# Gate products of a mixture-of-experts layer with the gate's weights standing, a bridge of unit-matrix products, and one more shared unit ahead of the routed ones

## The reference, cut to what matters

```python
t = layernorm(h).reshape(-1, d)                      # 3136 x 128
hs = gelu(einsum('td,nfd->ntf', t, sw1) + sb1)       # 2 shared experts, F = 512
shared = einsum('ntf,ndf->td', hs, sw2) + sb2.sum(0)
logits = t @ gate_w.T + gate_b                       # 3136 x 8
probs = softmax(logits)
top_v, top_i = top_k(probs, 2)
hr = gelu(einsum('td,efd->etf', t, rw1) + rb1)
oe = einsum('etf,edf->etd', hr, rw2) + rb2
routed = sum over the 2 chosen experts of top_v * oe
out = h + shared + routed
```

## Time and profile before

| | |
|---|---|
| median of 3 runs | 440.13 us (439.99 to 445.27) |
| profiled execution | 444.05 us, its span 442.1 us |
| PE busy | 364.2 us, 82% of the span |
| PEld, DVE, ACT, POOL busy | 299.8, 183.0, 205.5 and 174.1 us |
| granted clock, mean of the span | 0.883 |

### The profile page before, as it was taken

One profiled execution on the slowest core, in us unless ns is written; L12 is line 12 of the kernel. 1 busy time (PEld: TensorE's weight loads), 2 busy tenths in 40 slices (PEclk: granted clock), 3 DMA queues, 4 the chain that ended last, 5 costly groups with the idle time before them and its releaser, 6 DMA issues.

```text
span 442.1 us, 7120 instructions
## 1 busy us (share of the span) xinstructions
PE 364.2 (82%) x2490; PEld 299.8 (68%) x2490; DVE 183.0 (41%) x579; ACT 205.5 (46%) x424; POOL 174.1 (39%) x226
## 2 busy tenths in 40 slices
PE   0596998998967895839899999999999999989400
PEld 0465856666655784739777878988988988988300
DVE  0473485737769202392787221121121121121166
ACT  2660647837351631445563244554454445455153
POOL 7015134255221230062000357767767767654100
PEclk9995799998995697955798899999999999999855
DMA  8962046930010341022003015425435444455185
GB/s 209 265 191 74 16 131 165 312 128 0 1 71 40 122 150 60 1 74 73 0 33 130 19 42 210 159 101 212 156 128 183 161 146 166 172 173 187 29 278 149
DMA packets 22168, 54.38 MB, mean 123 GB/s; under 512 B 4551, under 2 KB 10109, under 8 KB 22137
## 3 DMA queue, kind: packets, MB, share of 16 engines
q1 hardware_dynamic: 17625, 46.25, 31.8%
q0 software_dynamic: 3968, 7.41, 6.0%
q10 hardware_dynamic: 544, 0.33, 0.4%
HBM read 28.10 MB, written 6.93 MB: 79 GB/s over the span
## 4 chain that ended last, share of the span: by engine, by line
PE 52%; issue 15%; DVE 12%; DMA 8%; POOL 4%; POOLq 3%; DVEq 3%; ACT 3%; SPq 1%; ACTq 0%
PE bank L1528 11%; PE bank L1505 11%; PE bank L1515 8%; DMA Xc<-in_x 3%; PE bank L1267 3%; PE bank L1300 3%; DVE dT L848 2%; PE bank L1480 2%; PE bank L1485 2%; PE bank L1486 2%; PE bank L1487 2%; DMA out<-osb 2%; DMA Tt<-kpad 1%; PE bank L1355 1%; PE bank L1563 1%
## 5 line engine op out<-in xcount | busy, mean ns | idle before, releaser
L633 POOL DMA_INDIRECT xg<-yd,take x56 | 54.5, 974 | 64.1 <-DVE give L1186 47.3
L784 ACT ACTIVATE gf<-bank,wb 128x256 f32<-128x256 f32 (+1 forms) x128 | 51.3, 447 | 52.6 <-PE bank L1505 52.6
L640 POOL DMA_INDIRECT rd<-og,give x56 | 55.2, 986 | 41.4 <-DVE og L1200 28.9
L1528 PE MATMUL bank<-wb,gf 128*128 128x128 f32 x448 | 55.4, 275 | 1.0 <-DVE og L1200 1.0
L1505 PE MATMUL bank<-x,wb 128*128 128x256 f32 (+1 forms) x256 | 54.0, 354 | 2.1 <-issue 1.2
L1528 PEld LDWEIGHTS bank<-wb,gf 128*128 128x128 f32 x448 | 53.2, 192 | 1.5 <-DVE og L1200 1.5
L784 ACT ACTIVATE gf<-bank,vcol 128x392 f32<-128x392 f32 x64 | 35.2, 588 | 36.5 <-PE bank L1487 36.5
L1505 PEld LDWEIGHTS bank<-x,wb 128*128 128x128 f32 x256 | 43.3, 191 | 9.3 <-issue 1.4
L1515 PE MATMUL bank<-gf,ws 128*128 128x392 f32 x128 | 44.8, 492 | 0.0
L1193 DVE COPY x<-bank 128x256 f32<-128x256 f32 (+1 forms) x32 | 12.5, 391 | 65.4 <-PE bank L1563 65.3
L1300 PE MATMUL bank<-patchT,Wp 128*128 128x392 f32 x96 | 38.4, 527 | 0.0
(11 more groups left out here) (266 smaller groups left out, 627.7 us busy)
## 6 DMA issues: line engine op xcount, KB each, us to landing
wb<-tab SPq DMA_DIRECT2D x32, 578.0 KB, 3.3
Xc<-in_x SPq DMA_DIRECT2D x12, 784.0 KB, 6.8
rk<-rd SPq DMA_DIRECT2D x8, 392.0 KB
Tt<-kpad SPq DMA_DIRECT2D x8, 300.1 KB
raw<-in_L_ffn_rw SPq DMA_DIRECT2D x1, 2048.0 KB, 10.2
out<-osb SPq DMA_DIRECT2D x8, 196.0 KB
Tt<-kpad SPq DMA_DIRECT2D x2, 600.2 KB
Tt<-kpad SPq DMA_DIRECT2D x1, 1200.5 KB
```

Of the source, the lines that this page charges most:

```text
L633: G.indirect_dma_start(out=xg[i % AHEAD][:, t, :], out_offset=None, in_=yd[:, :], in_offset=bass.IndirectOffsetOnAxis(ap=take[:, at:at + 1 ...
L640: G.indirect_dma_start(out=rd[:, :], out_offset=bass.IndirectOffsetOnAxis(ap=give[:, at:at + 1], axis=0), in_=og[i % 2][:, t, :], in_offse ...
L784: nc.scalar.activation(gf[q % 2][:, o, 0:width(q)], bank[o][:, 0:width(q)], ACT.Gelu, bias=bias1(n, o)).then_inc(act_done, 1)
L1528: last = MM(bank[7][:, D * t:D * (t + 1)], gf[q % 2][:, o, 128 * t:128 * (t + 1)], wb[i % WB][:, FO + F + o * D:FO + F + (o + 1) * D], sta ...
```

## The change

The gate's weights (`gwT`, 128 by 8) stand, and a chunk's 392 tokens move: one product a chunk instead of four. Its output is 8 rows, in one of four groups of 32 rows of a bank; four chunks share a bank. DVE copies each of the two banks to SBUF (`lgt`), TensorE transposes them, four transposes a bank, and DVE adds the bias in two instructions. Both copies stand in `choose()`, behind `low_y(0)`; the transposes stand between the last gate product and `up(0)`. 28 products of the unit matrix, whose result nobody reads, stand ahead of the first transpose of y. The wait for the expert weights moves ahead of the first gate product. `LEAD` is 7 and `S_TURN` is 4; `count_places()` stands behind `up(2)` instead of `up(1)`. With these constants, the last shared unit stands after block 26, and five routed blocks end the list.

```diff
+IDLE_Y = 28
-LEAD = 6
+LEAD = 7
-S_TURN = 3
+S_TURN = 4
+        lgt = [place(f"lgt{i}", [128, GT], "y") for i in range(2)]
             def choose():
-                dve.wait_ge(gate_done, NG)
-                V.tensor_tensor(lg[:, :, :], bank[7][0:PAIR, 0:NPAIR * E].rearrange("p (g e) -> p g e", e=E),
-                                gbb[:, :].unsqueeze(1).broadcast_to([PAIR, NPAIR, E]), ALU.add)
+                for b in range(2):
+                    dve.wait_ge(gate_done, 4 * (b + 1))
+                    V.tensor_copy(lgt[b][:, :], bank[b][:, 0:GT]).then_inc(lgt_ready, 1)
+                dve.wait_ge(logits_T, 2)
+                for b in range(2):
+                    V.tensor_tensor(lg[:, NPAIR // 2 * b:NPAIR // 2 * (b + 1), :].rearrange("t (c g) e -> t c g e", g=GP),
+                                    bank[4 + 3 * b][0:PAIR, :].rearrange("t (g c e) -> t c g e", g=GP, c=4)[:, :, :, 0:E],
+                                    gbb[:, :].unsqueeze(1).unsqueeze(1).broadcast_to([PAIR, 4, GP, E]), ALU.add).then_inc(logits_read, 1)
             def gate(c):
+                if c == 0:
+                    pe.wait_ge(w_hi, 2 * NX)
+                    pe.wait_ge(w_lo, NS)
                 pe.wait_ge(y_in, c + 1)
+                MM(bank[c // 4][32 * (c % 4):32 * (c % 4) + E, 0:GT], gwT[:, :], y32(c), start=True, stop=True,
+                   tile_position=(0, 32 * (c % 4))).then_inc(gate_done, 1)
+            def transpose_logits(b):
+                pe.wait_ge(lgt_ready, b + 1)
                 for g in range(GP):
-                    p = GP * c + g
-                    last = MM(bank[7][0:PAIR, p * E:(p + 1) * E], y32(c)[:, g * PAIR:(g + 1) * PAIR], gwT[:, :], start=True, stop=True)
-                last.then_inc(gate_done, 1)
+                    last = to_columns(bank[4 + 3 * b][0:PAIR, g * 128:(g + 1) * 128], lgt[b][:, g * PAIR:(g + 1) * PAIR])
+                last.then_inc(logits_T, 1)
             def down_shared(q):
+                if n == 0:
+                    pe.wait_ge(logits_read, 1)
+            for _ in range(IDLE_Y):
+                MM(bank[3][:, 0:D], ident[:, :], ident[:, :], start=True, stop=True)
             for c in range(NG):
                 transpose_y(c)
                 if c >= 1:
                     gate(c - 1)
             gate(NG - 1)
-            pe.wait_ge(w_hi, 2 * NX)
-            pe.wait_ge(w_lo, NS)
+            for b in range(2):
+                transpose_logits(b)
             up(0)
...
-                if q == 0:
+                if q == 1:
                     count_places()
```

More of the change, by code:

```diff
@@ L356, in tower @@
         y_ready = [sem(f"y_ready{i}") for i in range(2)]
-        gate_done, lg_ready, exp_ready, sel_ready, rank_T, rank_read = (sem(n) for n in (
-            "gate_done", "lg_ready", "exp_ready", "sel_ready", "rank_T", "rank_read"))
+        gate_done, lgt_ready, logits_T, logits_read, lg_ready, exp_ready, sel_ready, rank_T, rank_read = (sem(n) for n in (
+            "gate_done", "lgt_ready", "logits_T", "logits_read", "lg_ready", "exp_ready", "sel_ready", "rank_T", "rank_read"))
         sort_const, sort_tables, own_ready, hot_ready, inv_T, idx_ready = (sem(n) for n in (
```

## The result

| | median us (runs) | ratio to the kernel before, 95% interval |
|---|---|---|
| changed kernel, with the first result | 451.26 (4) | 1.0213 (1.0142 to 1.0283) |
| the same, timed again later | 450.40 (4) | 1.0234 (1.0171 to 1.0298) |

The kernel before had medians of 440.71, 440.50, 440.87 and 439.32 us in the four sets of runs, with single runs from 435.2 to 447.1. By the ratios the change makes the kernel 2.1 to 2.3% slower, 9.4 to 10.3 us. The ratios are of fast runs alone and the medians of all runs, so the differences of the medians (10.6 and 11.1 us) need not be the same.

The account below looks back on a forecast made before the run. PE was taken as the bound, by when it reaches the routed stage and how much of its list is done by then. Median 440.13 plus 8.5 us (7.5 to the first routed unit, 1.0 at the end) gave 448.6; range 443.0 to 453.5.

Parts of the forecast that it names:

- Bridge: Ahead of the first transpose of y: 28 products take 6.2 us, fit the 7.0 us pause, cost nothing.
- Rival E: Gate stage: clock falls before the products despite the 28 bridging products; part of the forecast, no separate chance given.
- Gate products: Gate stage: 0.66 us a product at full clock, ACT becomes the bound, products end at 207.3 us at best.
- Logits: Copies and transposes of the logits, new on the path: complete at 210.8 us against 211.48, gain 0.7 us.
- Counting behind `up(2)`: PE waits 3 us for low_y(1); with 1.2 us for a clock fall, the sort starts 3.4 us late.
- rival B: PE's list stays covered, clock stays up through up(2) and the seventh unit, tail neutral: about 444 us; chance 0.2.
- The wait that replaces the inverts: Before up(4): PE waits 7 us for low_y(2), inverts now behind down(3); with two still to do, 5.8 us behind.
- First routed unit: Start of the routed stage: 267.2 us, 7.5 us late, with bounds 4.7 and 11.
- The end: Last five routed blocks: 1.6 us of waits for weights, 0.6 us saved on the last sum; net 1.0 us lost.
- The sum: Whole kernel: 7.5 us to the first routed unit plus 1.0 us at the end, 8.5 us lost.
- C: Gate runs at half clock to its end: 3.7 us more on all behind the logits, 452.3 us; chance 0.15.
- A: Clock and earlier gate win about 5.5 us if low_y(2) is not late for PE: 434.6 us; chance 0.12.

Follow-up runs that it names:

- both low_y moved: Changed kernel with low_y(1) moved into choose() and low_y(2) ahead of sort_places on VectorE: 436.98 us, ratio 0.9895; timed again 436.52 us.
- the order alone: Kernel before with LEAD 7, S_TURN 4 and count_places behind up(2), old gate products, no bridge: 452.24 us, ratio 1.0253.
- low_y(2) moved: Changed kernel with low_y(2) moved ahead of sort_places on VectorE: 440.52 us, ratio 0.9996.
- the gate part alone: Changed kernel with LEAD 6, S_TURN 3 and count_places behind up(1), as before; new gate products and bridge stay: 440.44 us, ratio 0.9980.

## Why the prediction was right, point by point

*Bridge.* Right: 6.4 us, over at 192.80, the clock down again at 197.1 and up by 201. Rival E, that the clock falls all the same, was part of the forecast; in other profiles of kernels with the bridge it fell as late as 201.0, and in the first one with both low_y moved it did not fall in this stage at all. That the bridge gains nothing in the stages of this kernel is borne out by the experiment without it.

*Gate products.* Right: ACT became the bound, last product at 207.87 against 207.3 plus 0.5. For the changes of width I had taken 0.5 us in five; from start to start a gate product takes 0.75 us (203.92 to 204.67) where 0.66 would do (the estimate of the prediction), and four transposes behind it 0.49 (204.67 to 205.16) where 0.39 do between 193.59 and 193.98, so 0.1 us for each change. The drain that the Trainium skill states in "TensorEngine Tiling (Array Packing)", Key Properties, may stand behind it, but a cost of 0.41 us each is not what the trace shows here.

*Logits.* A gain of 1.3 us instead of 0.7.

*Counting behind `up(2)`: the step that failed in size.* The wait was 2.77 us, as said (3). But the clock stayed at 1.00, and I had put 1.2 us on its fall. With the earlier logits, the sort started at 222.02, 1.1 us late, not 3.4. So a sign that I had named for being right failed: the counts' product came at 221.71, before 222.5. Rows of before with 1.76 us of waiting at 1.00 spoke against a fall; rival B had read them rightly.

*The wait that replaces the inverts.* Right: 6.86 us for 7 (both its ends some 2 us earlier than forecast, so the 2 us of the step before cancel in it), the same wait with the order alone, and gone when low_y(2) moved.

*First routed unit.* 265.09 against 267.2: the 2.3 us of the step before, carried on. Late by 5.4, not 7.5; 5.5 by the second pair of profiles. Of the 5.4, about 3.5 are the two inverts still to do, 0.8 the half clock in `up(4)` and `down(3)`, and the rest is the unit between the two pairs of inverts: it took 6.90 us (247.24 to 254.14), in part at 0.50, where 5.0 are counted for it, while the stretch from the last invert to the first routed unit was 0.6 us shorter than before.

*The end.* 1.0 us was too little: 2.1 by the first pair of profiles, 1.1 by the second. The wait was 2.14, inside what I gave it, and the last transposed sum and its add no longer stand between the last two blocks, as forecast; half of the first pair's loss is the half clock behind the wait, which I had not priced. Over all profiles the end costs more: the mean back is 157.4 us in the eight with seven units ahead and the last shared unit behind block 26, 159.9 in the five with six; with the 5.0 us that is a loss of 2.5.

The sum: 7.5 and 6.6 us by the two pairs of profiles, against 8.5. The ratios say 9.4 and 10.3, with intervals from 6.3 to 12.5 and from 7.5 to 13.1 us. So 2 to 4 us are not located, or are the scatter of few runs; the profiles of the kernel before, 3.3 and 1.3 us above its medians, may have had long stages. What scatters ahead of the first transpose of y, 4.5 us in fourteen profiles, could hold some of it, but its means are alike: 194.2 us in the four profiles of kernels with the old gate, 194.4 in the ten others. The sign and the mechanism are shown, the last 2 us aren't. That 448.6 came within 3 us of 451.26 owes something to luck: the front was forecast 2.1 us too long, the end 1.1 us too short (first pair), and the rest is what no stage accounts for.

Of the rivals, C (a half clock to the end of the gate) did occur once, in the kernel with the gate part alone, where the logits came 2.7 us later, not 3.7 (the rows themselves gave 3.5: 2.6 for four products and 0.9 for two groups of transposes). A's condition, low_y(2) not late for PE, was met with low_y(2) moved, where the time was that of the kernel before, and with both moved, where the medians were 3.9 and 2.8 us lower; its 5.5 us were not reached.

## What to carry to other kernels

When a step is moved later on one engine, ask what the engine did in its old place: here two inverts covered a wait for another engine's list, and the wait was laid bare at full length. Look then at the other engine for a short instruction that waits for nothing and stands behind long ones; moving a 0.56 us subtraction was worth 10 us. And a unit of cover that is brought forward is missing where it stood.

## What the runs showed of the hardware that was not expected

- TensorE's granted clock can stay at 0.50 while PE is busy without a gap. Behind the bridge, with the old gate products (8 columns moving) between transposes, it did so from 201 to 211 us; with the new ones (392 columns moving) and no bridge it rose from 0.50 to 1.00 at 199.4 and 200.8 us, some 7 us behind the first transpose of y. But the form of the products doesn't settle it: in one profile with the new ones and the bridge it was 0.50 from 201 to 211 as well, and in another with the bridge it did not fall in this stage. What decides is not shown.
- The level differs from execution to execution at the same instruction. It moved the logits by 2.7 us among kernels whose gate stage is the same code (19.32 against 16.59 us), and the front of one kernel by 1.5 us; single runs of the kernel before spread over 12 us.
- Going between full-width transposes and products in a 32-column group costs about 0.1 us each way, not the 0.41 us for which the weight loads stood idle in the earlier trace rows.
